# First group of a fused decoder kernel: GpSimd's order, the weight loads, the fifth projection and the constants are moved

## The reference, cut to what matters

```python
x = x + mamba(layernorm(x))                      # the long part, in which the change lies
x = x + matmul(fake_quant(layernorm(x)), fake_quant(ctx))
x = x + ffn_with_experts(layernorm(x))

def mamba(x):                                     # x: 2 x 256 x 512
    h = rms_norm(x)
    gate, hBC, dt = split(h @ in_proj_w.T)        # 8192 gate, 8192 hidden + 8 groups of B and C, 128 heads
    hBC = silu(causal_conv(hBC, conv_w, conv_b))  # 4 taps
    dt = softplus(dt + dt_bias)
    cs = cumsum(-exp(A_log) * dt)                 # per head, over time
    M[i, j, head] = (C[i] . B[j]) * exp(cs[i] - cs[j])   # i >= j, else 0
    y = M @ (hid * dt) + Dp * hid
    y = group_norm(y * silu(gate)) * gnorm_w      # 8 groups of 1024 channels
    return x + y @ out_proj_w.T
```

## Time and profile before

| | us |
|---|---|
| median of 3 runs | 790.49 (790.13 to 791.45) |
| the profiled execution, its own time | 791.84 |
| span of its profile | 789.7 |
| busy of the span: PE / DVE / ACT / POOL | 774.6 / 636.4 / 596.5 / 696.3 |

### The profile page before, as it was taken

How to read it: one execution, slowest core, us unless ns; L and a number is a source line. 1 busy time by engine, 2 the same in 40 slices (tenths; PEclk the granted TensorE clock), 3 DMA queues, 4 the chain that set the end, 5 groups by cost and what they waited for, 6 DMA issues and landing times.

```text
span 789.7 us, 13488 instructions
## 1 busy us (share of the span) xinstructions
PE 774.6 (98%) x4275; PEld 611.2 (77%) x4275; DVE 636.4 (81%) x753; ACT 596.5 (76%) x1055; POOL 696.3 (88%) x553
## 2 busy tenths in 40 slices
PE   8989899999999999999999999999999999999997
PEld 7767677877887777877787777877787778877765
DVE  6888787888879886889779886888778778798875
ACT  5799677788778877788678877787687877788552
POOL 6689999899889998899889998999899998899551
PEclk9999999999999999999999999999999999999999
...
GB/s 327 119 159 209 91 135 101 128 135 133 67 160 133 133 111 115 133 131 127 74 160 127 116 99 131 135 113 129 109 133 116 122 123 100 136 114 66 1 2 54
DMA packets 58028, 94.94 MB, mean 120 GB/s; under 512 B 13168, under 2 KB 46064, under 8 KB 58000
## 3 DMA queue, kind: packets, MB, share of 16 engines
...
HBM read 93.26 MB, written 1.31 MB: 120 GB/s over the span
## 4 chain that ended last, share of the span: by engine, by line
PE 90%; POOL 4%; DVE 3%; ACT 2%; issue 1%; DMA 0%; DVEq 0%; POOLq 0%; ACTq 0%
PE ps_z L1222 25%; PE ps_out L1357 21%; PE ps_h L1222 21%; PE ps_y L1344 11%; PE ps_t L1195 4%; POOL win_lo L305 1%; PE ps_out L1195 1%; PE ps_t L1367 1%; DVE conv L814 1%; DMA acc<-in_x 0%; POOL csx L343 0%; POOL wout_lo L310 0%; POOL win_hi L296 0%; PE ps_h L1330 0%; PE ps_t L1330 0%
## 5 line engine op out<-in xcount | busy, mean ns | idle before, releaser
L305 POOL TENSOR_TENSOR win_lo<-w_raw,win_hi 128x1024 fp32r<-128x1024 f32 x64 | 182.0, 2843 | 9.7 <-DMA csx<-cs_rows 4.7
L604 ACT ACTIVATE decay<-csx,cs_own 128x256 f32<-128x256 f32 (+1 forms) x512 | 184.4, 443 | 0.8
L814 DVE SCALAR_TENSOR_TENSOR conv<-ps_h,par,conv 128x510 f32<-128x510 f32 (+2 forms) x192 | 142.9, 744 | 20.0 <-ACT conv L533 15.4
L604 ACT ACT_TABLE_LOAD x63 | 80.8, 1283 | 90.0 <-PE ps_y L1344 82.0
L899 DVE TENSOR_TENSOR decay<-decay,cbm 128x1536 f32<-128x1536 f32 x64 | 145.5, 2273 | 0.3 <-ACT decay L604 0.3
L343 POOL TENSOR_SCALAR_AFFINE_SELECT csx<-csx 128x512 f32<-128x512 f32 x128 | 109.3, 877 | 2.5 <-DMA csx<-cs_rows 2.5
L958 DVE SCALAR_TENSOR_TENSOR v<-hidT,par,ps_y 128x512 f32<-128x512 f32 x64 | 47.8, 747 | 78.3 <-PE ps_y L1344 78.2
L1357 PE MATMUL ps_out<-wout_hi,y_hi 128*128 128x512 f32 x252 | 100.3, 398 | 0.0
L1344 PE MATMUL ps_y<-decay,hid_dt 128*64 128x256 f32 (+1 forms) x1024 | 97.3, 332 | 2.4 <-DVE decay L899 1.3
L1357 PE MATMUL ps_out<-wout_lo,y_hi 128*128 128x512 f32 x252 | 99.6, 395 | 0.0
L1357 PE MATMUL ps_out<-wout_hi,y_lo 128*128 128x512 f32 x252 | 99.3, 394 | 0.0
...
## 6 DMA issues: line engine op xcount, KB each, us to landing
...
csx<-cs_rows SPq DMA_DIRECT2D x128, 256.0 KB, 3.5
...
par<-in_wpar SPq DMA_DIRECT2D x64, 4.0 KB, 3.6
...
```

Of the source, the lines that this page charges most:

```text
L305: eng.tensor_tensor(win_lo[:, r2, :], w_raw[:, r4, 0:W_IN], win_hi[:, r2, :].bitcast(f32), ALU.subtract).then_inc(low_win, 1)
L604: done = eng.activation(decay[:, r2, b, h, lo:lo + n], csx[:, r2, b, h, lo:lo + n], ACT.Exp, bias=cs_own[:, r2, t, h:h + 1])
L814: eng.scalar_tensor_tensor(out=out_b[:, :, back:], in0=src_b[:, :, 0:S - back], scalar=w[:, TAPS - 1 - back:TAPS - back], in1=out_b[:, :, ...
```

## The change

It touches only the code for the first group, on four engines.

- GpSimd: in slot 1, `win_lo` of pair 3 waits for mask(1). win(4) moves from slot 3 to the end of slot 1 and waits for mask(2); `wout_lo` of pair 1, which stood there, goes behind sel(3) in slot 2. `wout_lo` of pair 2 waits for mask(3). In slots 4 to 7, sq(s) and wout(s) go ahead of sel(s+1), and win(s+1) ahead of own(s+1). In slot 3, wout(3) goes ahead of sel(4).
- SP: w(4) to w(7) are issued one slot sooner, ahead of the rows of pairs 3 to 6.
- TensorE: in slot 3, h(4) is issued behind out(3) and ahead of scan(3); in slot 4 it is left out. A wait for `low_wout` is added ahead of the output projections.
- VectorE: `constants()` moves from the end of slot 0 to the end of slot 1, behind conv(2).

```diff
@@ SP
-                if not (first and k < 4):
+                if not first:
...
+                if first and 3 <= k < PPG - 1:
+                    eng.dma_start(par[:, k + 1, :], wpar_d[s + 1]).then_inc(w_in[(k + 1) % 4], 16)
+                    eng.wait_ge(low_wout, s - 2)
+                    eng.dma_start(w_raw[:, (k + 1) % 4, :], wmain_d[s + 1]).then_inc(w_in[(k + 1) % 4], 16)
@@ GpSimd, slot 1
                     split_in(3, 1)
+                    eng.wait_ge(dve_m, 1)
                     lower_in(3, 1, 4)
                     eng.wait_ge(csx_in[0], 64)
                     select(0)
                     split_out(1)
-                    lower_out(1, 2)
+                    eng.wait_ge(w_in[0], 64)
+                    eng.wait_ge(pe_gate, 3)
+                    eng.wait_ge(dve_m, 2)
+                    split_in(0, 0)
+                    lower_in(0, 0, 5)
                     return
@@ GpSimd, slot 2
                     select(1)
+                    lower_out(1, 2)
                     split_out(2)
+                    eng.wait_ge(dve_m, 3)
                     lower_out(2, 3)
@@ GpSimd, slots 3 to 7
+                if first:
+                    if k > 3:
+                        eng.wait_ge(w_in[n4], 32 * ((k + 1) // 4 + 1))
+                        eng.wait_ge(pe_gate, s)
+                        split_in(n4, 1 - r2)
+                        lower_in(n4, 1 - r2, s + 2)
+                    eng.wait_ge(act_exp, s)
+                    own_sums(s + 1, 1 - r2)
+                    if k > 3:
+                        eng.wait_ge(pe_out, s - 3)
+                    sum_squares(s, g, k, first)
+                    split_out(r4)
+                    lower_out(r4, s + 1)
+                    eng.wait_ge(csx_in[1 - r2], 32 * ((k + 1) // 2 + 1))
+                    select(1 - r2)
+                    if k == 4:
...
+                        lower_bc(2)
+                    return
@@ VectorE
-                    constants()
                     return
                 if first and k == 1:
                     scale_hidden(1, 1)
                     mask(1, 0, 1)
                     conv_hidden(2, 2)
+                    constants()
                     return
@@ TensorE, slots 0 to 3
-                if k < 3:
-                    eng.wait_ge(low_win, k + 2)
-                    eng.wait_ge(dve_conv, 3 * k + 3)
-                    project(ps_h[:], win_hi[:, 1 - r2, 0:KT * P], win_lo[:, 1 - r2, 0:KT * P], pe_hid)
-                else:
+                if k == 3:
                     project_out(3, 0, 3)
+                eng.wait_ge(low_win, k + 2)
+                eng.wait_ge(dve_conv, 3 * k + 3)
+                project(ps_h[:], win_hi[:, 1 - r2, 0:KT * P], win_lo[:, 1 - r2, 0:KT * P], pe_hid)
@@ TensorE, project_out
+                if isinstance(s, int):
+                    eng.wait_ge(low_wout, s - 2)
```

More of the change, by code:

```diff
@@ L381, in slot @@
                     select(1)
+                    lower_out(1, 2)
                     split_out(2)
+                    eng.wait_ge(dve_m, 3)
                     lower_out(2, 3)
                     return
-                if k == 3 and not first:
+                if first:
[14 more added lines that the diff above has]
+                    if k == 4:
+                        eng.wait_ge(bc_in, 16 * 2)
+                        eng.wait_ge(pe_bc, 2)
+                        eng.tensor_scalar(wbc_hi[:], bc_raw[:, 0:BC_W], 1.0, 0.0, ALU.mult, ALU.add).then_inc(hi_wbc, 1)
+                        lower_bc(2)
+                    return
+                if k == 3:
                     eng.wait_ge(pe_out, s - 3)
@@ L404, in slot @@
                     split_in(n4, (k + 1) % 2)
-                    if first:
-                        lower_in(n4, (k + 1) % 2, s + 2)
-                        eng.wait_ge(csx_in[1 - r2], 32 * (4 * g + (k + 1) // 2 + 1))
-                    else:
-                        eng.wait_ge(csx_in[1 - r2], 32 * (4 * g + (k + 1) // 2 + 1))
-                        lower_in(n4, (k + 1) % 2, s + 2)
+                    eng.wait_ge(csx_in[1 - r2], 32 * (4 * g + (k + 1) // 2 + 1))
+                    lower_in(n4, (k + 1) % 2, s + 2)
                     select(1 - r2)
@@ L1256, in slot @@
                     return
-                eng.wait_ge(low_win, s + 1)
-                eng.wait_ge(dve_conv, 3 * s)
-                if k == 1:
-                    eng.wait_ge(dve_cb, 2 * g + 1)
-                project(ps_h[:], win_hi[:, r2, 0:KT * P], win_lo[:, r2, 0:KT * P], pe_hid)
+                if not (first and k == 4):
+                    eng.wait_ge(low_win, s + 1)
+                    eng.wait_ge(dve_conv, 3 * s)
+                    if k == 1:
+                        eng.wait_ge(dve_cb, 2 * g + 1)
+                    project(ps_h[:], win_hi[:, r2, 0:KT * P], win_lo[:, r2, 0:KT * P], pe_hid)
                 if turned:
```

2 lines of the change are left out of this document (1 added, 1 removed).

## The result

| | before | changed |
|---|---|---|
| median, us (4 runs each) | 790.66 (790.13 to 791.45) | 795.47 (795.26 to 795.96) |
| ratio, 95% interval | | 1.0048 [1.0025, 1.0072] |
| the profiled execution / its span | 791.84 / 789.7 | 795.3 / 793.3 |

The changed kernel is 4.8 us slower by the medians; the recorded ratio is 1.0048, 0.5%, a little less than that of the two medians (1.0061). 796.6 was forecast.

A forecast was written before the change was run, and what follows sets the result against it. PE, busy 774.6 of 789.7 us, was taken to bound the kernel. Turn(6) +4.3 and clock +1.86 summed to +6.2, 796.7 on the median; forecast 796.6, 8-in-10 range 789.0 to 799.0, the forecast's own 794.5 to 798.5.

The forecast's parts named there:

- The mechanism: GpSimd: 3.8 us idle ahead of win(4), and sq(5), wout(5) ahead of sel(6), make turn(6) 4.3 us late.
- clock behind turn(6): PE: after waiting 5.7 us at turn(6) the granted clock falls, slowing the projections behind it by 1.86 us.
- First slots: PE and VectorE: scan(1) 1.3 us earlier at 39.0, that gain gone at scan(2), 48.0 against 47.85 before.
- VectorE's share of the port: GpSimd, mask(2) to sel(6): VectorE wants 11.7 us of the shared port; sel(6) taken to end at 89.5.
- Sel(4): GpSimd: sel(4) ends near 63.3, after 11.4 us of GpSimd's work and 4 of VectorE's; turn(4) at 70.0.
- Turn(5): PE: sel(5) ends at 74.5, dec(5) follows, hid(5) ends at 82.3, so turn(5) starts at 82.3 against 79.04.
- The transfers: SP: rows of pair 4, behind w(5), land near 60.5; cost nothing, or 0.5 to 1 us. w(4) before 45.
- GpSimd keeps ahead: Rival: VectorE's instructions fall in GpSimd's shadow, sel(6) ends near 79 to 80, no turn late: 784.5; chance 0.15.
- Slower without the clock: Rival: turn(6) late by 3 to 4.5, waits in pieces, slowing no longer or hidden: 793.5 to 795; chance 0.20.
- Worse: Rival: pair 4's rows late, clock falls at turn(4) to turn(6), GpSimd pays all VectorE's work: 798.5 to 801; chance 0.07.
- Nothing changes: Rival: sel(6) ends near 85.2, turn(6) stays where it was, clock loss stays: 789 to 792; chance 0.08.
- The lock rule: GpSimd and VectorE: first starter holds the shared port pair; mask waits would save up to 2.4 us, not certain; sum unaffected.

The follow-up runs named there:

- e1: Changed kernel with sel(s+1) right behind own(s+1), ahead of sq and wout, in slots 3 to 7; 793.18 us, ratio 1.0023.
- e2: Kernel before with only GpSimd's new order in slots 4 to 7 (win, own, sq, wout, sel last); 793.39 us, ratio 1.0022.
- e10: Changed kernel with sel behind own, constants at end of slot 3, `wout_lo` of pair 1 back in slot 1; 789.27 us, ratio 0.9973.
- e6: Kernel before with only w(4) to w(7) issued one slot sooner; 791.14 us, ratio 1.0012.
- e5: Changed kernel with TensorE's old order, scan(3) behind out(3) and h(4) behind turn(3); 795.95 us, ratio 1.0063.
- e3: Changed kernel without GpSimd's wait for mask(2) ahead of win(4); 795.43 us, ratio 1.0045.
- e9: Changed kernel with the constants moved from the end of slot 1 to the end of slot 3; 794.51 us, ratio 1.0041.
- e12: The changed kernel run again, nothing altered, beside new runs of the kernel before; 795.98 us, ratio 1.0054.
- e7: Changed kernel with sel(s+1) right behind own(s+1) and without the wait for mask(2); 791.96 us, ratio 1.0017.
- e8: Kernel before with GpSimd's split of B's and C's weights at the end of slot 5 instead of slot 4; 791.82 us, ratio 1.0019.

## Why the prediction was right

**The mechanism holds, in both its parts.** Late sel by the order of slots 4 and 5: taken back (e1), 2.9 of the 4.8 us in the traces go, 3.1 in the medians over before in the same comparison (4.8 and 1.7); put alone into the kernel before (e2), it costs 2.0. The idling ahead of win(4): with the order of e1 in place, filling it and freeing mask(2) of the constants (e10) takes another 3.3 (76.29 and 73.04 to turn(7); 1.7 over before and 1.6 under it). These 3.3 hold a third share that can't be parted from them, that of the rows of pair 4, for which sel(4) waited 1.89 us in e1 and not at all in e10. Neither the weights a slot sooner in the kernel before (e6), nor the fifth projection's place (e5), nor the wait for mask(2) by itself (e3) shows a difference in the time, though without that wait turn(6) comes 1 us sooner. In e9 the constants alone carry about 1.5.

| step | predicted | measured, aligned |
|---|---|---|
| scan(1) | 39.0 | 39.10 |
| constants | 1.7 | 1.69 |
| scan(2) | 48.0 | 47.83 |
| GpSimd idle ahead of win(4) | 3.8 | 4.16 |
| z(4) | 60.2 | 60.03 |
| rows of pair 4 waited for | 0, or 0.5 to 1 | 0.51 |
| sel(4) ends | 63.3 | 64.1 |
| turn(4) | 70.0 | 70.84 |
| sel(5) ends | 74.5 | 72.5 |
| turn(5) | 82.3 | 82.72 |
| sel(6) ends | 89.5 | 88.3 |
| turn(6) | 98.2 | 97.0 |
| clock behind turn(6) | 1.86 | 1.75 |
| sum | +6.2 | +4.8 |

**First slots.** All of it came as worked out. The gain at scan(1) was gone at scan(2).

**The term that was mis-sized** is VectorE's share of the port between mask(2) and the end of sel(6). From 47.06 to 87.42 are 40.36 us; less GpSimd's own 31.1 and the 0.51 for the rows of pair 4, 8.75 remain, where I put 10.5. The whole of VectorE's demand was 11.7 and the kernel before showed 9.2 paid. I took a value nearer to the full price because GpSimd would have fewer pauses. The rows don't bear that out. Counted instruction by instruction, as the prediction did for before, eleven of GpSimd's are longer than undisturbed, by 9.1 us in sum, against 9.2 (the 31.1 are some 0.3 too many). And VectorE pays too, which the sum left out: its four masks, four `y_lo` and four `yg` of this stretch are 5.4 us longer than undisturbed (8.5 before), `y_lo` for one with 1.89 and 2.21 us instead of 0.74. With 9.2 in the sum, sel(6) would have been forecast at 88.2, turn(6) at 96.9 and the time at 795.3.

**Sel(4).** It waited 0.51 us for its rows, took 2.81 us for the 1.22 of its undisturbed two instructions, beside mask(4), and ended 0.8 later than forecast. Turn(4) was 2.1 later than before and yet PE waited 3.55 for it, since PE had come 1.6 sooner by its gain at z(4).

**Turn(5): the right number for another reason, in this trace.** The prediction held it up by dec(5). In the trace hid(5) ends at 79.62 and the turn starts at 81.87, without a wait for it: sel(5) was 2 us earlier than forecast, and PE itself was the late one, by its wait at turn(4) and by the clock at 0.50 behind that. The prediction had the clock fall only behind turn(6). The extra fall changed nothing in the sum, because PE had to wait for hid(6) anyway, 3.91 instead of the 5.7 forecast. The second trace (e12) has it as the prediction did: turn(5) waits for hid(5), the clock falls only at turn(6), and the wait there is 5.67; but turn(5) is 1.8 late, not 3.3. (The forecast for sel(5) has a slip in its sum: 47.9, 19.7 and 7.1 make 74.7, not 74.5.)

**The transfers.** The rows of pair 4 cost their half microsecond at sel(4), as the term's upper side said; no change of a turn beyond that is seen. w(4) was there in time: in e3, where GpSimd goes for it at once, it has landed by 44.63 against a forecast of before 45.

**The rivals.** *GpSimd keeps ahead* asked that VectorE's work fall in GpSimd's shadow: it did not. *Slower without the clock* had the waits in pieces, as they came (at turn(4) and turn(6)), but the clock fell, and the 1.75 us of it are what lies between this rival and the time measured: 795.47 − 1.75 = 793.7. *Worse* wanted the clock to fall at three turns and the whole of VectorE's work paid; it fell at two and 8.75 of 11.7 were paid. *Nothing changes* wanted sel(6) near 85.2; it ended at 88.3.

**The lock rule.** `win_lo` of before, for which mask(1) went ahead though it had been issued 0.45 us later, stayed an exception. In e7 `win_lo` began 0.97 us ahead of mask(2) and the mask took 3.31 us; in e3 mask(2) began 0.48 us ahead of `win_lo`, at 45.31, and took 2.00, `win_lo` 3.75. By the Trainium skill, "SBUF — State Buffer", section "SBUF: two separate sides", the pair of ports goes to whichever instruction starts first, for its whole length: these two rows agree with that, the row of before does not, and what decided there stays open. (The 0.25 us that mask(2) of e3 took beyond its 1.75 fit the end of `win_hi` of pair 4, which ran until 45.70.)

**What stays open.** How the 1.8 us of e1 over before divide between the idling, the constants and the rows of pair 4 is known only through kernels that change all three (e10) or keep the late sel (e9). Why runs of before, e7 and e8 spread by several us and those of the changed kernel and of e10 (789.1 to 790.7) by less was not tried.
